# The chain from the reloaded rows to the FFN in two parts of 256 rows, in an attention and FFN kernel on one core

## The reference

```
x = x + layernorm(attention(layernorm(x)))
x = x + layernorm(ffn(layernorm(x)))
```

## Time and profile before

| | |
|---|---|
| median of 3 runs | 1006.89 us (1006.85 to 1008.29) |
| the profiled execution | 1008.13 us |
| its span, first to last instruction | 1006.4 us |
| PE busy | 908.8 us (90%) |
| DVE busy | 838.3 us (83%) |
| POOL busy | 726.6 us (72%) |
| ACT busy | 626.4 us (62%) |
| mean granted TensorE clock | 0.962 |

### The profile page before, as it was taken

The page is one execution under the profiler, slowest core; times in us unless marked ns, Lnnn a source line. Parts: engine busy times, 40 slices in busy tenths (PEclk is TensorE's granted clock), DMA queues, the critical chain, the costliest instruction groups (busy, mean ns, idle before and its releaser), DMA issues. The chain is left out here.

```text
span 1006.4 us, 18403 instructions
## 1 busy us (share of the span) xinstructions
PE 908.8 (90%) x6503; PEld 708.1 (70%) x6503; DVE 838.3 (83%) x1201; ACT 626.4 (62%) x1058; POOL 726.6 (72%) x582
## 2 busy tenths in 40 slices
PE   3626628999999999999999999999999999999996
PEld 3424418777777777877777777777787777777773
DVE  6898898899899999999999989999999989353122
ACT  2745825867586767766686758676776665452431
POOL 3556656798879886998789877988699888552333
PEclk9866968999999999999999999999999999999999
DMA  6011050014102320114002410232011302220001
GB/s 179 0 43 42 1 125 1 1 42 110 39 2 64 85 64 0 28 51 116 13 1 62 99 47 0 63 83 63 1 28 53 76 14 64 55 52 1 22 2 42
DMA packets 78320, 46.14 MB, mean 46 GB/s; under 512 B 39609, under 2 KB 72377, under 8 KB 78265
## 3 DMA queue, kind: packets, MB, share of 16 engines
q1 hardware_dynamic: 73400, 45.10, 17.1%
q10 hardware_dynamic: 4864, 0.32, 0.3%
HBM read 28.63 MB, written 16.78 MB: 45 GB/s over the span
## 5 line engine op out<-in xcount | busy, mean ns | idle before, releaser
L1134 DVE TENSOR_TENSOR prod<-ps_x,qkvl 128x2048 f32<-128x2048 f32 x128 | 290.8, 2281 | 10.6 <-ACT ps_x L789 6.7
L653 PE MATMUL ps_gate<-xhi,wg 128*128 128x256 f16 x1024 | 230.5, 273 | 2.3 <-DVE xlo L1253 1.7
L653 PE MATMUL ps_up<-xhi,wu 128*128 128x256 f16 x1024 | 230.5, 273 | 0.0
L653 PE MATMUL ps_up<-xlo,wu 128*128 128x256 f16 x1024 | 230.5, 273 | 0.0
L653 PE MATMUL ps_gate<-xlo,wg 128*128 128x256 f16 x1024 | 230.5, 273 | 0.0
L859 ACT ACTIVATE gact<-ps_gate,sgate 128x256 f32<-128x256 f32 x256 | 106.9, 468 | 158.8 <-PE ps_gate L653 157.2
L1028 POOL TENSOR_TENSOR flo<-fuse,fhi 128x512 f16<-128x512 f32 x128 | 148.8, 1163 | 77.6 <-ACT fhi L865 77.6
L968 POOL TENSOR_TENSOR sum<-prod 128x1024 f32<-128x1024 f32 x64 | 150.6, 2363 | 40.3 <-DVE prod L1134 37.5
L1262 DVE SCALAR_TENSOR_TENSOR fuse<-ps_up,sup,gact 128x256 f32<-128x256 f32 x256 | 110.1, 471 | 82.6 <-PE ps_up L653 70.7
L977 POOL TENSOR_TENSOR sum<-prod 128x1024 f32<-128x1024 f32 x64 | 151.6, 2371 | 19.5 <-DVE prod L1134 12.9
L673 PE MATMUL ps_acc<-wd,fhi 128*128 128x512 f16 x512 | 153.3, 379 | 0.0
(11 more groups left out here) (152 smaller groups left out, 1401.6 us busy)
## 6 DMA issues: line engine op xcount, KB each, us to landing
xb<-in_L_attn_x SPq DMA_DIRECT2D x64, 128.0 KB, 2.7
xr<-in_L_attn_x SPq DMA_DIRECT2D x16, 512.0 KB
attn_rows<-ratt SPq DMA_DIRECT2D x16, 512.0 KB, 3.5
o<-attn_rows SPq DMA_DIRECT2D x32, 256.0 KB, 4.2
out_x<-y SPq DMA_DIRECT2D x15, 512.0 KB
x<-in_L_ffn_w_gate SPq DMA_DIRECT2D x1, 1024.0 KB, 5.3
xr<-in_L_ffn_w_up SPq DMA_DIRECT2D x1, 1024.0 KB, 8.4
out_x<-y SPq DMA_DIRECT2D x2, 256.0 KB
```

The source lines that it names most:

```text
L653: mm = nc.tensor.matmul(ps[:, HALF * i:HALF * i + HALF], w[:, k, P * j:P * j + P], xs[:, k, rows], start=(k == 0 and part == 0), stop=(k = ...
L1134: nc.vector.tensor_tensor(prod[:, half].rearrange("p (s j k) -> p s j k", j=WIN, k=WIN), left[:, :, None, :].broadcast_to([P, 4 * WIN, WIN ...
```

## The change

1. `ffn_norm1`, `norm1_add`, `ffn_norm2` and `norm2_apply` become (t, hi): each works on two of the four blocks, with semaphores of its own for each norm. `warm_fx` waits for `xr_sum` of 2 (two blocks summed) and issues 12 products; `warm_cat` is gone.
2. `cent_out`'s scaling by the weight and its addition of the token are done in two halves of 8 channels each, scale and add by turns, in place of one scaling of all 16 channels and two additions.
3. `keep_x1` also waits for all four blocks of `xr_sum`.
4. `START` is empty, its steps stand in `BEFORE`, and `BEFORE`, `STEADY` and `ENDING` have a new order. Shown here: the end of `BEFORE`, and the steps of the chain in the others.

```diff
-            def warm_cat(at, bank):
-                pe.wait_ge(sum_done, 2 * UNITS * (2 * at[0] + at[1]) + 7)
-                warm(0, 8, bank)
-
             def warm_fx(t, bank):
-                pe.wait_ge(f_stats, 2)
-                warm(0, 8, bank)
+                pe.wait_ge(xr_sum, 2)
+                warm(0, 12, bank)
...
-            def norm2_apply(t, bank):
-                act.wait_ge(f_rs, 2 * t + 2)
-                for q in range(NQ):
+            def norm2_apply(t, hi, bank):
+                act.wait_ge(n2_rs, 2 * t + hi + 1)
+                for q in (2 * hi, 2 * hi + 1):
...
-            def ffn_norm2(t, bank):
-                dve.wait_ge(xr_sum, NQ * t + NQ)
-                row_stats(xr, 1, range(NQ), fst, f_chain, 2 * t + 2, f_stats)
+            def ffn_norm2(t, hi, bank):
+                dve.wait_ge(xr_sum, NQ * t + 2 * hi + 2)
+                row_stats(xr, 1, (2 * hi, 2 * hi + 1), fst, n2_chain, 2 * t + hi + 1, n2_stats)
...
+        def scale_and_add(eng, queue, n, g):
             token = xl[:, g].rearrange("p h (c t) -> p h t c", c=C)
+            rows = cent[:].rearrange("p h t c -> p (h t) c")
             for hi in range(2):
                 c = slice(HB * hi, HB * hi + HB)
+                eng.tensor_tensor(rows[:, :, c], rows[:, :, c], lnw[:, None, c].broadcast_to([P, WIN * WIN, HB]),
+                                  ALU.mult).then_inc(lnw_chain, 1)
+                queue.wait_ge(lnw_chain, 2 * n + hi + 1)
```

The start and the end of `BEFORE` (p, a, b, c are the halves (0, 0), (0, 1), (1, 0), (1, 1)):

```diff
-        START = [("ln1_apply", 0, 0), ("blocks", 0), ("ln1_stats", 0), ("ln1_fin", 0), ("scale_sums", 0),
-                 ("scale_row", 0), ("xt", p, 0, 0), ("scale_pow2", 0), ("scale_spread", 0), ("xt", p, 0, 1),
...
-                  ("qkv", c, 1, 0), ("qx", c, 0), ("qkv", c, 1, 1), ("ffn_norm1", 0), ("xt", c, 1, 1),
-                  ("qkv", c, 1, 2), ("pv_sum", b, 2), ("qkv", c, 1, 3), ("att_store", 0), ("recip", b),
-                  ("norm1_add", 0), ("ffn_norm2", 0), ("attn_out", b), ("norm2_apply", 0), ("warm_fx", 0),
-                  ("warm_cat", a), ("pv_sum", b, 3), ("qk", c, 0), ("qk", c, 1), ("qx", c, 1), ("fx", 0, 0, 0),
-                  ("fx", 0, 0, 1), ("ln1_stats", 2), ("qk_sum", c, 0), ("load_xb", 2), ("cat", b, 0)]
+        START = []
+
+        BEFORE = [("ln1_apply", 0, 0), ("blocks", 0), ("ln1_stats", 0), ("ln1_fin", 0), ("scale_sums", 0),
+                  ("ln1_apply", 0, 1), ("scale_row", 0), ("scale_pow2", 0), ("xt", p, 0, 0), ("scale_spread", 0),
...
+                  ("qx", c, 0), ("ffn_norm1", 0, 0), ("pv", b, 3), ("ffn_norm1", 0, 1), ("qkv", c, 1, 0),
+                  ("recip", b), ("xt", c, 1, 1), ("pv_sum", b, 2), ("qkv", c, 1, 1), ("qkv", c, 1, 2),
+                  ("qkv", c, 1, 3), ("norm1_add", 0, 0), ("norm1_add", 0, 1), ("ffn_norm2", 0, 0), ("pv_sum", b, 3),
+                  ("attn_out", b), ("qk", c, 0), ("norm2_apply", 0, 0), ("qx", c, 1), ("warm_fx", 0),
+                  ("fx", 0, 0, 0), ("load_xr", 0), ("fx", 0, 0, 1), ("ffn_norm2", 0, 1), ("att_store", 0),
+                  ("cat", b, 0), ("load_xb", 2), ("qk", c, 1), ("ln1_stats", 2)]
```

More of the change, by code:

```diff
@@ new lines, in sandwich_kernel @@
+        ENDING = [(0, ("qk", a, 2)), (0, ("qx", c, 0)), (0, ("load_xr", 1)), (0, ("cat", p, 1)),
+                  (0, ("softmax", b, 0)), (0, ("proj", p, 0)), (1, ("qk_sum", a, 0)), (1, ("square", p, 0)),
+                  (2, ("xt", c, 0, 1)), (2, ("qk", a, 3)), (2, ("norm2_apply", 0, 1)), (2, ("qkv", b, 1, 3)),
+                  (2, ("ln1_apply", 2, 1)), (2, ("proj", p, 1)), (2, ("square", p, 1)), (3, ("qk_sum", a, 1)),
+                  (3, ("qk_sum", a, 2)), (3, ("cent_var", p)), (3, ("recip", b)), (4, ("cent_std", p)),
+                  (5, ("softmax", a, 0)), (5, ("cent_out", p)), (5, ("fx", 0, 1, 0)), (6, ("xt", b, 0, 0)),
+                  (6, ("exp", a, 0)), (6, ("qk", b, 3)), (6, ("qk_sum", a, 3)), (6, ("qkv", c, 0, 0)),
+                  (7, ("qkv", c, 0, 3)), (8, ("softmax", a, 1)), (10, ("finish", -1, 1)), (12, ("qkv", b, 1, 1)),
+                  (13, ("pv", a, 0)), (13, ("finish_apply", -1, 1)), (13, ("exp", a, 1)), (13, ("pv", a, 1)),
+                  (13, ("xt", c, 1, 1)), (14, ("qkv", b, 0, 2)), (14, ("pv_sum", a, 0)), (14, ("ln1_apply", 2, 0)),
+                  (15, ("attn_out", b)), (16, ("finish_add", -1, 1)), (16, ("pv", a, 2)), (17, ("ln1_fin", 2)),
+                  (17, ("pv_sum", b, 2)), (17, ("pv", b, 2)), (17, ("pv_sum", b, 3)), (18, ("xt", b, 1, 1)),
+                  (18, ("pv_sum", a, 1)), (18, ("att_store", 1)), (18, ("recip", a)), (18, ("pv", a, 3)),
+                  (19, ("token_bias", c)), (19, ("pv_sum", a, 2)), (20, ("qkv", b, 0, 1)), (21, ("pv_sum", a, 3)),
+                  (21, ("qx", b, 1)), (21, ("attn_out", a)), (21, ("fx", 0, 1, 1)), (22, ("qkv", b, 0, 0)),
+                  (24, ("xt", c, 1, 0)), (24, ("cat", a, 0)), (24, ("xt", b, 1, 0)), (25, ("cat", a, 1)),
+                  (25, ("proj", a, 0)), (25, ("keep_x1", 0)), (26, ("proj", a, 1)), (26, ("square", a, 0)),
+                  (26, ("square", a, 1)), (27, ("qkv", c, 0, 1)), (28, ("cent_std", a)), (28, ("cent_var", a)),
+                  (30, ("cent_out", a)), (31, ("qk", b, 0)), (31, ("exp", b, 1)), (32, ("qkv", b, 0, 3)),
+                  (34, ("ln1_stats", 3)), (34, ("finish", 0, 0)), (35, ("qk", b, 2)), (37, ("qk", c, 0)),
+                  (38, ("xt", b, 0, 1)), (38, ("ffn_norm1", 1, 0)), (38, ("ffn_norm1", 1, 1)), (39, ("pv", b, 3)),
+                  (39, ("norm1_add", 1, 0)), (40, ("exp", b, 0)), (40, ("qkv", b, 1, 0)), (40, ("qk", c, 1)),
+                  (40, ("load_xb", 3)), (40, ("qkv", c, 1, 0)), (41, ("softmax", b, 1)), (41, ("pv", b, 1)),
+                  (41, ("pv_sum", b, 0)), (42, ("pv_sum", b, 1)), (42, ("ffn_norm2", 1, 0)), (42, ("qk_sum", b, 1)),
+                  (42, ("qkv", c, 1, 1)), (43, ("pv", b, 0)), (43, ("qkv", b, 1, 2)), (43, ("norm2_apply", 1, 0)),
+                  (44, ("norm1_add", 1, 1)), (44, ("fx", 1, 0, 0)), (44, ("cat", b, 0)), (44, ("fx", 1, 0, 1)),
+                  (45, ("qk", b, 1)), (45, ("ffn_norm2", 1, 1)), (46, ("qx", c, 1)), (46, ("qk_sum", b, 3)),
+                  (46, ("qkv", c, 0, 2)), (47, ("token_bias", b)), (47, ("qkv", c, 1, 2)), (47, ("qk_sum", b, 2)),
+                  (47, ("qk_sum", b, 0)), (47, ("finish_add", 0, 0)), (47, ("qkv", c, 1, 3)),
+                  (47, ("finish_apply", 0, 0)), (47, ("xt", c, 0, 0)), (47, ("qx", b, 0))]
@@ L880, in keep_x1 @@
                 need(act, y_sum, NQ * t)
+                act.wait_ge(xr_sum, NQ * t + NQ)
                 if isinstance(t, int) and t == 0:
```

206 lines of the change are left out of this document (86 added, 120 removed).

## The result

The changed kernel is slower, by 0.5%: 1012.96 us median (1010.68 to 1015.39, 6 runs) against 1007.82 (1006.85 to 1008.68, 6 runs) of the kernel before on the same chip, a ratio of 1.0054 with a 95% interval of 1.0044 to 1.0064. The forecast was 1002.8, and its range ended at 1006.8. The first gate did come earlier. What ate the gain is a wait of PE at six tile boundaries.

A forecast was written before the change was run, and what follows sets the result against it. PE bounds the kernel behind the first gate; ahead of it DVE's ordered work, then a chain across engines. 1008.13 - 4.9 + 1.2 + 1.1 - 1.5 = 1004.0 for the profiled execution, 1002.8 against the median; range 999.2 to 1006.8.

The forecast's parts named there:

- At no cost: Boundaries other than tile 6's, and the changed DMAs and semaphores: no wait to lose and nothing added, put at 0.
- C: Rival, tile boundaries: the second half's `norm2_apply` in slot 2 waits for POOL, PE behind ACT; slower, 1011.2; chance 0.09.
- The chain: From `norm1_add` to the first gate: shortens by 4.1 us, from 14.59 to 10.45, bounds 3.0 and 5.
- T: Start of `norm1_add` ahead of the first gate: 0.8 us earlier in sum, bounds -6.5 and +3.
- Item (1): Part of T: DVE's eight `ln1_apply` ahead of `scale_pow2`, on which PE's second transpose waits; 0.4 us later.
- Item (3): Part of T: `cat` (a, 0) ahead of two `qkv` of b; the delay still ends in POOL's 2.4 us; no change.
- SP's own order is unchanged: Part of T, ahead of the first gate: SP's loads and store keep their order, so the o1 rows are no limit.
- What the gate takes over: Behind the first gate: DVE owes 7.0 us instead of 3.4, partly absorbed; cost 0 to 3.6, taken 1.2.
- The clock: At the first gate or just after: 1.2 GHz for some 3.3 us; cost 0 to 2.9 us, taken 1.1.
- Rival D: First gate: twelve products don't raise the clock; at most 1.8 us, 1004.6; counted within the forecast's chance of 0.58.
- The boundary of tile 6: End of tile 6: `fx` in slot 44 of `ENDING` removes the gate's 1.7 us wait for `xlo`; -1.5 us.

The follow-up runs named there:

- e2: The changed kernel with `norm2_apply` (1, 0) in `STEADY` moved behind the last two `qkv` of c: 1007.81 us, ratio 1.0011.
- e9: The changed kernel with only its tile boundary reordered (`norm2_apply`, second `ffn_norm2`, `fx` pair and `cat` (b, 0), five steps moved): 1006.01 us, ratio 0.9979.
- e8: The changed kernel with the edits of e2, e4 and e5, and `cat` (b, 0) of the first tile behind the first gate: 1006.49 us, ratio 0.9990.
- e10: The changed kernel with e9, e5 and e4, and `cat` (b, 0), `proj` (p, 0), `cat` (p, 1) in slot 1 of the first tile: 1000.89 us, ratio 0.9935.
- e5: The changed kernel with `cat` (a, 0) and (a, 1) behind `qx` (b, 1), and `xt` (a, 1, 1) directly behind `xt` (a, 1, 0): 1009.26 us, ratio 1.0018.
- e4: The changed kernel with six more products on PE between `fx` and `cat` ahead of the first gate: 1011.23 us, ratio 1.0043.
- e12: e10 without any product in front of the first gate, neither the twelve nor the six: 1022.11 us, ratio 1.0146.
- e13: e12 with 18 products put back far ahead of the first gate, at about 56 us: 1004.76 us, ratio 0.9977.
- e1: The changed kernel with both `fx` of the next tile's first 256 rows in slot 46 of `STEADY`, not 44: 1021.22 us, ratio 1.0141.

## Why the prediction was wrong

**The step that failed: "At no cost. The other boundaries have no wait to lose."** They had none to lose, and got one. The new order of `STEADY` was costed as DMAs and semaphores of SP; ACT's order was not followed. In it `norm2_apply` moved from slot 44 to 42 and two `qkv` from slot 40 to 42 and 43, so it now stands ahead of two evictions for whose banks PE waits. A term that was put at 0 measured 7.8 us at six boundaries. e2 gives back 4.3 of it by moving this step alone, and e9 all of it by order alone. The rows to see it were in the rival's own text: POOL busy for 9.54 of 10 us at that place, so a `row_std` that ACT needs early comes late.

**The rival that was nearest, C, named the wrong instruction.** It put the wait at the second half's `norm2_apply` in slot 2, and there nothing waits. It had the shape right: ACT behind a full POOL, PE behind ACT, at seven boundaries. It said "at 1.2" it would be 1011.2; it was 1.3 at six (7.8/6), and 1013.0. A chance of 0.09 was too little for a mechanism with a full engine in it. The five slots of slack that spoke against it were counted for the second half only.

**The chain: right.** T + 10.45 was forecast for the gate, and some T + 8.2 for the work that `xhi` waits for; it is T + 11.06 and T + 8.33. The 0.6 that the gate is late is the wait of `cat` (b, 0) for POOL, which the forecast left out though the diff has that step ahead of the gate. Placed behind the gate (e8, e10), it no longer delays the gate, but the work behind it.

**T: wrong by 1.7**, 148.04 against 146.3; within its bounds. Item (1), 0.4 later, is not borne out: DVE's first product came 1.0 earlier (27.68), but over all traces it comes at 27.6 to 29.1 in the new order and at 28.3 to 28.8 in the old, so its sign is open. Item (3), "no change", failed: `cat` (a, 0) ahead of two `qkv` holds PE for 4.6, DVE's wait behind it is 4.8 where POOL's had been 2.4. "SP's own order is unchanged" failed too: the order is, but `load_xb` waits for `xt` (a, 1, 1), which moved, and starts at 58.42 instead of 52.57: 1.9 us on DVE. e5 undid both and gained 2.7 at the gate, 3.8 counted from DVE's first product.

**What the gate takes over: overestimated.** 1.2 was taken for DVE's debt. From the gate to 183 us PE is busy for 23.86 of 23.90 us, against 20.86 of 21.27 before: `qk` (c, 1) and the statistics were absorbed. The lead of 2.6 at the gate is still 2.7 in slot 8, so the first tile gave nothing back.

**The clock: right in size.** 1.1 was taken, 0 to 2.9 allowed. The profiled run lost nothing, and half of the runs are some 3 us longer at a lower mean clock; 1.9 of that is seen at the gate in e9's trace. One reading was off: the last pause of PE ahead of the old gate is 1.07 us, not 0.6, with a `cat` behind it; nothing in the sum hangs on it. The Trainium skill's rule from "TensorE: Matmul & The Clock Gate", Part 1, that the point of the rise moves from run to run against the kernel's start, agrees with the two traces under e4: the same code and order up to the gate, and the gate at 1.00 in one and at 0.50 in the other. Rival D is contradicted in its plain form. Without any product in front the gate runs at 0.50 (e12, e13), with twelve in three of seven traces at 1.00, and with the six more in all five.

**The boundary of tile 6: right.** -1.5 forecast, -2.1 measured, and the wait for `xlo` is gone.

The account: -2.6 at the gate, +7.8, -2.1 make +3.1 of the span's +3.0. The medians are 5.1 apart. Of the other 2.1, some 1.3 is an estimate for which runs lie in the middle: with half of its runs long, the changed kernel's middle span is 1010.4, 1.0 above the profiled one, while the profiled run of before lies 0.3 above its median. The rest, some 0.8, is time outside the span (2.6 against 1.7), which I have not followed.

## What to carry to other kernels

When an order by hand changes, walk it once for each engine and ask of each instruction that waits what stands behind it, and who needs that. The profile names the instruction behind (an eviction); the cause is one ahead. A step whose input comes from the fullest engine belongs behind everything on its own engine that others need. And the repair begins with the step that waits (e2: -5.1 us), not with the one that suffers (e1: +8.3 us).

## What the runs showed of the hardware

A loop's time can change with code that stands outside it. Eighteen products fewer ahead of the loop (36 matmuls and 36 weight loads in the trace, as each product runs as two halves) cost 17 us (e12 against e13). PE then stood for 11.1 us at the three jumps back, and 27 packets of code were fetched where there is one or none. A tile in the loop has 808 matmuls and 807 weight loads by e10's trace.

The Trainium skill, "Runtime: NRT & Kernel Launch", section "Instruction fetch mechanics", states that PE's instruction memory holds 2048 instructions and is refilled in blocks of 16 KiB, 256 instructions, and that a taken branch to code outside the current window of two blocks has to wait for a fetch. The packets agree in size (33 in 0.54 MB in e13, 16.4 KB each), and so does the place of the stops, at the jumps back. The window of two blocks doesn't agree: every jump back over 1615 instructions would then stop PE, and e10, e13 and the kernel before show no such stop. That 1615 instructions, with their waits and branches, fit into 2048 or not by how they lie across the blocks is the likely mechanism. The runs show the packets, the stops and the cure by 18 products, not the borders of the blocks.
